# A decoder layer on one core: the steps of all five engines in a new written order, and a few more explicit waits

## What is computed

```
x = layernorm(x + attention(x))              # windows of 128 rows, 16 heads of 16
x = layernorm(x + ssm(ctx, z = x))           # ctx: 512 rows of 256
x = layernorm(x + feed_forward(x))

attention:  x @ Wc + bc; q, k, v; scores*scale + rel_bias[j - i]; softmax; probs @ v; @ Wd + bd
ssm:        xp = in_proj_w @ ctx^T (512 channels); causal convolution with 4 taps; u = silu(. + conv_b)
            x_dbl = x_proj_w @ u -> dt_lo (16 rows), Bm (16 rows), Cm (16 rows)
            delta = softplus(dt_proj_w @ dt_lo + dt_proj_b);  A = -exp(A_log)   # 512 channels x 16 states
            state_n = state_n * exp(delta * A_n) + (delta * u) * Bm_n           # over the 512 rows, n = 0..15
            y = sum_n state_n * Cm_n + D * u;   out = y * silu(z)
feed_forward: xq = round(127/max|x| * norm(x)) clipped;  g = silu(xq @ sign(W_g)^T)
            u = xq @ sign(W_u)^T;  (g * u) @ sign(W_d)^T     # inner width 2048
```

## Time and profile before

| | |
|---|---|
| runs | 957.9 to 962.74 us, median 962.4 us of 3 |
| profiled execution | span 964.3 us, its own time by the page (1.9 us above the median) |
| VectorE (DVE) | 852.1 us busy, 88% of the span |
| TensorE (PE) | 836.9 us, 87% |
| ScalarE (ACT) | 682.8 us, 71% |
| GpSimd (POOL) | 445.2 us, 46% |
| DMA | 43.93 MB, 46 GB/s in the mean |
| chain that ended last | DVE 50%, PE 27%, issue 15%, ACT 6% of the span |

### The profile page before, as it was taken

The page is one execution under the profiler, slowest core; times in us unless marked ns, Lnnn a source line. Parts: engine busy times, 40 slices in busy tenths (PEclk is TensorE's granted clock), DMA queues, the critical chain, the costliest instruction groups (busy, mean ns, idle before and its releaser), DMA issues.

```text
span 964.3 us, 12713 instructions
## 1 busy us (share of the span) xinstructions
PE 836.9 (87%) x4258; PEld 526.9 (55%) x4258; DVE 852.1 (88%) x1168; ACT 682.8 (71%) x1148; POOL 445.2 (46%) x260
## 2 busy tenths in 40 slices
PE   6979787788888898999889888999889899884997
PEld 3447566574455565655456555654456556563453
DVE  2499999998899999999999999898989999987554
ACT  4875655665897788866897888766878788772532
POOL 2065745542265755553356655454345655453000
PEclk9995867789989989999998999899979998977999
DMA  8222252320101111001001111001000010000000
GB/s 228 79 71 82 75 180 85 101 64 0 46 23 34 66 36 36 29 1 56 13 23 34 67 43 34 22 1 35 11 23 33 23 43 31 28 12 0 12 22 23
DMA packets 29216, 43.93 MB, mean 46 GB/s; under 512 B 6128, under 2 KB 10096, under 8 KB 29152
## 3 DMA queue, kind: packets, MB, share of 16 engines
q1 hardware_dynamic: 26512, 42.52, 13.9%
q10 hardware_dynamic: 2640, 0.59, 0.3%
HBM read 38.78 MB, written 4.33 MB: 45 GB/s over the span
## 4 chain that ended last, share of the span: by engine, by line
DVE 50%; PE 27%; issue 15%; ACT 6%; POOL 1%; DMA 1%; DVEq 0%; POOLq 0%; ACTq 0%
DVE h L1519 18%; DVE acc L1536 12%; DVE s_pT L1402 3%; PE bank_a L2274 3%; PE bank_f L2422 3%; DVE neg_max L1408 2%; PE bank_m L2398 2%; PE bank_f L2499 2%; DVE p_lo L1600 2%; PE bank_a L2301 2%; DVE g_p L1596 2%; DVE h L1451 2%; PE bank_m L2362 2%; DVE st L1422 2%; PE bank_a L2319 1%
## 5 line engine op out<-in xcount | busy, mean ns | idle before, releaser
L524 POOL TENSOR_TENSOR b_x<-u,b_row 128x1024 f32<-128x1024 f32 x124 | 340.3, 2753 | 263.1 <-DVE h L1519 261.9
L1519 DVE TENSOR_TENSOR_SCAN h<-d_a,b_x 128x1024 f32<-128x1024 f32 x128 | 292.5, 2302 | 0.0
L2398 PE MATMUL bank_m<-ident,h 128*128 128x128 f32 x1024 | 173.8, 304 | 47.9 <-DVE acc L1536 41.9
L1536 DVE SCALAR_TENSOR_TENSOR acc<-bank_m,c_cols,acc 128x512 f32<-128x512 f32 x256 | 186.1, 740 | 6.5 <-PE bank_m L2398 5.3
L893 ACT ACTIVATE d_a<-delta,a_neg 128x511 f32<-128x511 f32 x256 | 168.6, 712 | 28.6 <-DVE h L1519 28.1
L2398 PEld LDWEIGHTS bank_m<-ident,h 128*128 128x128 f32 x1024 | 130.8, 158 | 89.7 <-DVE acc L1536 44.7
L936 ACT ACT_TABLE_LOAD x46 | 59.0, 1283 | 46.2 <-PE bank_f L2422 45.9
L512 POOL TENSOR_TENSOR rs<-ve,neg_half 128x1 f32<-128x1 f32 (+1 forms) x36 | 30.9, 859 | 131.0 <-DVE neg_mean L1617 70.5
L814 ACT ACTIVATE s_pT<-s_pT,neg_max 128x128 f32<-128x128 f32 x256 | 81.5, 390 | 11.9 <-DVE neg_max L1408 11.4
L2301 PE MATMUL bank_a<-k_par,qT 32*128 32x256 f32 x256 | 80.1, 436 | 2.5 <-DVE s_pT L1402 1.3
L2319 PEld LDWEIGHTS bank_a<-v_aug,s_pT 128*128 128x128 f32 x512 | 73.7, 220 | 8.3 <-issue 6.3
(11 more groups left out here) (182 smaller groups left out, 1458.5 us busy)
## 6 DMA issues: line engine op xcount, KB each, us to landing
b_row<-bc_rows SPq DMA_DIRECT2D x64, 256.0 KB, 3.2
x_next<-in_x_dram SPq DMA_DIRECT2D x4, 1024.0 KB, 5.7
y<-in_L_ffn_W_g_dram SPq DMA_DIRECT2D x16, 256.0 KB, 2.7
xn<-in_L_ffn_W_u_dram SPq DMA_DIRECT2D x16, 256.0 KB, 3.0
g_p<-in_L_ffn_W_d_dram SPq DMA_DIRECT2D x16, 256.0 KB, 3.2
out_dram<-y SPq DMA_DIRECT2D x16, 256.0 KB, 2.7
cx<-in_ctx_dram SPq DMA_DIRECT2D x4, 512.0 KB, 5.2
acc<-n_L_xattn_in_proj_w_dram ACTq DMA_DIRECT2D x1, 512.0 KB, 5.3
```

The source lines that it names most:

```text
L524: nc.gpsimd.tensor_tensor(b_x[:, half], du[:, halves(half)], b_row[:, n % 2].unsqueeze(1).to_broadcast([P, EH, S]), ALU.mult)\
L1519: nc.vector.tensor_tensor_scan(flat(h[:, (n + 1) % 2, halves(half)]), flat(d_a[:, half]), flat(b_x[:, half]), 0.0, ALU.mult, ALU.add).then ...
L1536: nc.vector.scalar_tensor_tensor(acc[:, i], bank_m[bank][:], c_cols[:, i, bass.ds(n, 1)], acc[:, i], ALU.mult, ALU.add).then_inc(m_free[ba ...
L2398: last = tr(bank_m[bank][:, c * P:(c + 1) * P], h[:, (n + 1) % 2, c, i * P:(i + 1) * P], ident[:])
```

## The change

The functions and the calls are the same; the order of the calls is new on all five engines, and a few waits are added. Instead of `opening`, `tile_first`, `first_seam`, `tile(b, w)`, `seam(b)` and `ending`, each engine has `first_front`, `batch_0` to `batch_3` and `last_feed_forward`, every call written out, so that the order no longer repeats from batch to batch or from window to window. No instruction's operands, sizes or buffers change.

The added waits, in `du_1` (POOL) and alike `du_0` (DVE), `round_rows` (ACT), `scan` and `quantise` (DVE):

```diff
             def du_1(b):
-                pool.wait_ge(a_full[2], (2 * TT + 1) * b + 1)
+                for full, use in ((f_full[0], f_skip(b)), (f_full[1], f_skip1(b)), (f_full[2], FC + b if b else 0),
+                                  (a_full[2], (2 * TT + 1) * b)):
+                    pool.wait_ge(full, use + 1)
...
             def round_rows(n, t):
 
                 act.wait_ge(q_step, Q_STEPS * n + Q_STEPS)
+                if n:
+                    act.wait_ge(xq_ready, n)
                 nc.scalar.activation(xn[:], x2b[:, t], ACT.Identity, bias=round_col[:, 0:1], scale=q_mul[:, 0:1])\
                     .then_inc(xn_ready, 1)
                 act.wait_ge(xn_ready, n + 1)
+                if n > (B - 1) * TT:
+                    act.wait_ge(tail_xq, n - (B - 1) * TT)
+                elif n:
+                    act.wait_ge(f_full[1], f_seams(n - 1) + F1_TILE * (n - 1) + 1)
                 nc.scalar.activation(xq[:], xn[:], ACT.Identity, bias=round_col[:, 1:2]).then_inc(xq_ready, 1)
...
                 dve.wait_ge(da_ready, 2 * (DS * b + n) + half + 1)
+                if n >= 2:
+                    dve.wait_ge(m_full[1], M_BATCH * b + M_FRONT + 2 * (n - 2) + 2)
                 nc.vector.tensor_tensor_scan(flat(h[:, (n + 1) % 2, halves(half)]), flat(d_a[:, half]),
                                              flat(b_x[:, half]), 0.0, ALU.mult, ALU.add).then_inc(h_ready, 1)
...
                 dve.wait_ge(rsq_ready, b + 1)
                 dve.wait_ge(x2_ready, TT * b + t + 1)
+                if n:
+                    dve.wait_ge(q_step, base)
...
                 dve.wait_ge(q_step, base + 3)
+                if n:
+                    dve.wait_ge(xn_ready, n)
                 nc.vector.tensor_scalar(q_mul[:], q_rec[:], Q_MAX, None, ALU.mult).then_inc(q_step, 1)
```

SyncE. The weight blocks come in another order, and `spread` of eight pairs of rows stands in reverse, as in batch 1 (first lines) and batch 3; the stores stand elsewhere:

```diff
+                spread(1, 10)
+                next_rows(2)
+                spread(1, 12)
+                spread(1, 11)
+                spread(1, 14)
+                spread(1, 13)
+                spread(1, 15)
+                store(0, 1)
...
+                spread(3, 3)
+                spread(3, 5)
+                spread(3, 4)
+                spread(3, 7)
+                store(1, 3)
+                spread(3, 6)
```

GpSimd. The `inputs` stand in the same order among themselves; `add_out_bias(0, 1)` to `(0, 3)` move from behind the `inputs` of rows 5 and later to the front, in front of `du_1(0)`:

```diff
+            def first_front():
                 pad(0)
                 column_constants()
                 add_out_bias(0, 0)
+                add_out_bias(0, 1)
+                add_out_bias(0, 2)
+                add_out_bias(0, 3)
                 du_1(0)
                 inputs(0, 0, 1)
+
+            def batch_0():
...
```

ScalarE. `sign(0, 0, 1)` is now the fifth step of all, and `context_columns(0, 1)` the first:

```diff
+            def first_front():
+                context_columns(0, 1)
                 context_columns(0, 0)
-                context_columns(0, 1)
                 taps_in(0, 0)
                 taps_in(0, 1)
+                sign(0, 0, 1)
                 front_columns()
                 taps_in(0, 2)
                 silu_u(0, 0)
                 taps_in(0, 3)
                 silu_u(0, 1)
-                silu_u(0, 2)
...
```

VectorE. The front runs its convolutions nearly as before; from there on the scans stand at other distances. Before, in the text of `seam(b)` for all batches, and after, in `batch_2` for the start of batch 2:

```diff
-                scan(b + 1, 0, 0)
-                add_bias(b + 1, 0, 0)
-                product(row(b + 1, 0), 0)
-                quantise(row(b + 1, 1), b, 1)
-                row_max(b + 1, 0, 0)
-                add_bias(b + 1, 0, 1)
-                low(row(b + 1, 0), 0)
-                scan(b + 1, 0, 1)
-                scan(b + 1, 1, 0)
-                product(row(b + 1, 0), 1)
-                gather(b + 1, 0, 0)
-                add_bias(b + 1, 0, 2)
-                row_max(b + 1, 0, 1)
-                low(row(b + 1, 0), 1)
-                row_max(b + 1, 0, 2)
-                gather(b + 1, 0, 1)
-                scan(b + 1, 1, 1)
-                gather(b + 1, 0, 2)
-                add_bias(b + 1, 0, 3)
-                product(row(b + 1, 0), 2)
-                gather(b + 1, 0, 3)
-                scan(b + 1, 2, 0)
-                gather(b + 1, 1, 0)
-                row_max(b + 1, 0, 3)
...
+                scan(2, 0, 0)
+                add_bias(2, 0, 0)
+                product(4, 0)
+                row_max(2, 0, 0)
+                quantise(5, 1, 1)
+                low(4, 0)
+                scan(2, 0, 1)
+                add_bias(2, 0, 1)
+                row_max(2, 0, 1)
+                scan(2, 1, 0)
+                product(4, 1)
+                gather(2, 0, 0)
+                add_bias(2, 0, 2)
+                row_max(2, 0, 2)
+                gather(2, 0, 1)
+                low(4, 1)
+                scan(2, 1, 1)
+                add_bias(2, 0, 3)
+                gather(2, 0, 2)
+                gather(2, 0, 3)
+                scan(2, 2, 0)
+                product(4, 2)
+                row_max(2, 0, 3)
+                gather(2, 1, 0)
+                gather(2, 1, 1)
+                low(4, 2)
+                scan(2, 2, 1)
+                gather(2, 1, 2)
+                gather(2, 1, 3)
+                scan(2, 3, 0)
+                add_bias(2, 1, 0)
+                gather(2, 2, 0)
+                product(4, 3)
+                row_max(2, 1, 0)
+                gather(2, 2, 1)
+                scan(2, 3, 1)
+                quantised_T(5)
+                gather(2, 2, 2)
...
```

3808 lines of the change are left out of this document (2496 added, 1312 removed).

## The result

The changed kernel takes 1018.55 us (median of 4 runs, 1014.24 to 1021.8); the kernel before, run beside it, 962.57 us. The ratio is 1.0558, with a 95% interval of 1.0488 to 1.0628: 56 us slower, where 25 were forecast. The direction was right, the size by half; the time lies 15 us above the top of the range (1003).

The account below looks back on a forecast made before the run. VectorE's queue was taken to bound 821.5 us, between a front chain, a short gap and a TensorE tail. Terms 0 + 0 + 32 + 2 - 9 = +25 on the 964.3 us span gave 989.3, as a median 987.4 us; range 960 to 1003.

Parts of the forecast that it names:

- the scans' lock: Scans 0.5 to 1.9 us behind another wait for POOL's `inputs`, each 2.38 us less its gap: +32 us, bounds 7 to 36.
- order wins: Rival, chance 0.11: POOL fails to get in front of scans due within 1.9 us, the idle saved decides: 956 us.
- no change: Rival, chance 0.07: the queues are in effect as before, as the instructions are the same ones: 962 us.
- Absorbed: Rival, chance 0.18: blocked scans stand where VectorE would have waited anyway, or POOL is late; half counts: 973 us.
- The stalls: VectorE's idle time between first scan and last gate multiply: the new order fills most of it, -9 us, bounds -20 and +6.
- if DVE's waits for PE's transposes grow beyond 6 us: Sign that the forecast is wrong: VectorE waiting more than 6 us for TensorE's transposes.
- clock too: Rival, chance 0.04: blocked VectorE idles TensorE, whose granted clock falls toward 0.76, adding 16 us of stalls: 1004 us.
- PE busy unchanged: Sign for the forecast: TensorE's busy time stays as before, with its tail at 67 us.
- The front: Before the first scan: an earlier `sign` waits for weights, and POOL's `add_out_bias` meets convolutions: +2 us, bounds +1.3 and +4.4.
- Waits: Added waits in `scan`, `quantise`, `round_rows` and the `du` steps are already met when reached: 0, upper bound about 3 us.
- SP's reversed rows: Eight pairs of `spread` in reverse order on SP; the delay, at most 10.8 us, is hidden behind VectorE's work: 0.
- The tail: The end set by TensorE takes the same 67 us in any order that keeps it fed: 0, bounds -1 and +2.

Follow-up runs that it names:

- the split inputs: Changed kernel with each of POOL's `inputs` as four instructions of 128x256 instead of one of 128x1024: 1004.35 us; the same split in the old order: 976.43 us.
- Taking the lock away: Changed kernel with POOL's `inputs` on only 64 of the 512 rows of each block, the rest left out: 995.52 us, ratio 1.030 to the kernel before.
- new_light: Changed kernel, with TensorE in batch 0 transposing only one of the four blocks of each state group: 1005.62 us, ratio 1.045 to the kernel before.
- new_pe_min: Changed kernel, TensorE in batch 0 doing one of four state and probabilities transposes and one of two score and value matmuls: 997.14 us, ratio 1.034.
- old_light: Order of the kernel before with the added waits, TensorE in batch 0 transposing one of four blocks of each state group: 965.83 us, ratio 1.001.
- old_pe_min: Order of the kernel before, TensorE in batch 0 doing one of four state and probabilities transposes and one of two score and value matmuls: 961.9 us, ratio 0.996.
- the seven waits: Changed kernel with seven of batch 0's `weights_T` steps, where TensorE waited 15.2 us, moved down by one to five other steps on TensorE: 1020.67 us, ratio 1.061.
- new_paired: Changed kernel with 25 scans on VectorE moved up by one to three instructions, directly behind the scan before: 1044.99 us, ratio 1.082 to the kernel before.
- old_unpaired: Order of the kernel before, with the second scan of 25 adjacent pairs on VectorE moved down by two instructions: 1016.34 us, ratio 1.055.

## Why the prediction went right and wrong

**The bound, and the scans' lock: right.** 34 short gaps were counted and 35.6 us worked out, 32 taken; the trace has 34.6 us more in the scans. By a little luck: the counted pairs gave 28.6 us, below the 32, and late `inputs` in front of other scans 8.0, which no term had. The price of 2.38 less the gap held pair by pair, though before the change it had been seen for a scan only near its end (0.2 us). The rule of the Trainium skill, page "SBUF — State Buffer", section "SBUF: two separate sides" (a lock held for the instruction of whichever engine starts first), is borne out by the split inputs: 4.14 us became 2.52. The lower bound, 7 us in all, and the rivals "order wins" and "no change" fell with it.

**How much of it reaches the end: half seen.** The forecast let all 32 through. Taking the lock away gave back 23 to 25 us. "Absorbed" had the mechanism, blocks that stand where VectorE would have waited, at half; about two thirds came through, with a margin of 7 us.

**The stalls: the step that failed.** The prediction put -9 us for stalls that the new order heals, between -20 and +6, and noted 13 gathers with little work since their bank came free, but gave them no price. In batches 1 and 3 it was right (idle time 7.3 to 6.1 and 13.5 to 6.5), the stalls of the earlier trace rows did go, and batch 2 rose a little (10.4 to 12.1). In batch 0 it was wrong by its sign: 10.0 to 30.7. The reason is in how the work was read, by VectorE's own order alone. The steps' counts and VectorE's work in front of each landmark were the same, so TensorE was taken to keep up as before. But in batch 0 it had been near the limit all along: the earlier trace rows has it at 130.5 of 157.9 us (83%) there at 0.76 of the clock. The runs show that TensorE's time bounds that batch in the new order (new_light, new_pe_min) and not in the old (old_light, old_pe_min). What in the new order leaves it less room was not isolated: the seven waits were not it. That two engines, each above 80% busy and waiting for each other, overlap less when one of their orders changes is the reading that fits new_paired and old_unpaired too, but it is argued. The prediction's own sign for this, "if DVE's waits for PE's transposes grow beyond 6 us", is what happened: 5.3 to 22.8.

**The clock: priced too low and too narrowly.** The rival "clock too" (0.04, 1004 us) had the direction: 0.91 fell to 0.876 over the span, and in batch 0 from 0.81 to 0.71, 80 to 138 us at the lower level. The prediction's sign "PE busy unchanged" did not hold: 836.9 became 857.0 us, with 21.3 more in batch 0 alone. But it was to be set off by the blocked scans, and it was not: with the lock away, batch 0 kept 120 us at the lower level and 26 us of its loss.

**The front: +2, measured -2.0.** ScalarE's early `sign` did wait for its weight block, until 19.88 us, and the next `taps_in` began at 21.09 instead of 19.98, 1.1 later where 1.8 was worked out. `first_input` started at 54.38 instead of 52.27, 2.1 later; that all of it comes from `sign` is not shown. What the prediction missed: `first_input` is now ahead of `du_1` by 0.25 us and takes 1.22 us, so the block of 2 us is gone from VectorE; and three weight copies and one `skip_in` moved behind the first scan, which makes the landmark sooner and not the work less. The sign of it is no chance of one run: the first scan starts at 55.5 to 59.4 us (median 56.4) in the eleven traces with the new front and at 56.8 to 59.5 (median 59.0) in the nine with the old.

**Waits, SP, tail: right.** The added waits are 0 (bounds 0 to 3, measured 1.000 [0.998, 1.002]); the 0.1 us a wait of the upper bound comes from no row, and no run shows any such cost. SP's reversed rows made POOL wait 27.0 us for a row, in five places, nearly all hidden; in one, at 799.2 us, the late `inputs` blocked a scan for 1.66. The tail was put at 0 with bounds -1 and +2; its stretch is 1.4 us shorter, and alone it is worth nothing measurable.

**The sum** was 0 + 0 + 32 + 2 - 9 = +25. By the profiled executions the 48.2 us are: -2.0 to the first scan, -1.4 in the tail, and 51.6 in the four batches, of which 33.6 are what the scans have over 2.28 us each (36.7 less 3.1), 14.2 idle time of VectorE (55.4 less 41.2) in place of -9, and 3.8 other busy time, mostly the steps that moved behind the first scan. One term, the stalls, carries the miss: 23 us of it. The range could not hold it: its top, 1003, is 41 above 962.4, the full 36 of the lock and +4 in front with nothing from the stalls. Even the prediction's own upper bound of +6 for them was not in it, and no term stood for TensorE.

## What to carry to other kernels

When only an order changes, count for each long instruction what stands between it and its forerunner on every engine that shares a port or a buffer with it; a gap a little shorter than the other engine's instruction costs what is missing, and a gap of nil costs nothing. Then do the same for what long, independent instructions cover: a scan that needs nothing new from the other engines is slack for them, and moving 25 of them by two places cost 53 us here, twice what the lock did. Where two engines are both above 80% busy in a stretch and wait for each other, do not forecast gains from a new order out of one engine's list; the second engine's time at the clock it is granted there is the bound to check first.

## What the runs showed of the hardware

POOL's four instructions of 128x256 took about 0.7 us each when nothing was in their way (2.11 us for three), against 2.37 for one of 128x1024, so some 0.15 us of each is fixed. The granted clock of TensorE fell with thinner work and rose with denser: 148 us at the lower level in batch 0 with a quarter of the state transposes, 52 us with four matmuls of 512 columns added to each group, in stretches of 229.0 and 240.7 us. A lower clock need not cost time: old_pe_min ran 141 us of batch 0 at half clock in 209.3 us, where before ran 80 us at half clock in 209.7. Where TensorE is the bound, as in batch 0 of the new order, these runs do not exclude that it does.
